# Tower of a language model: the state's product with the low part of the output weights over 128 rows instead of 64

## The reference, cut to what matters

```python
x = x + ssm(layernorm(x, ln1_s, ln1_b), A_diag, B, C, D)
h = layernorm(x, ln2_s, ln2_b)
x = x + gelu(h @ w1 + b1) @ w2 + b2

def ssm(x, a_diag, Bm, Cm, Dm):
    a = sigmoid(a_diag)              # 64 states
    u = x @ Bm                       # 256 -> 64
    # H[t] = a * H[t-1] + u[t], over the 512 tokens
    return H @ Cm + x @ Dm           # 64 -> 256 and 256 -> 256
```

## Time and profile before

| what | value |
|---|---|
| median of three runs | 2568.11 us (2562.83 to 2569.23) |
| the profiled execution | 2563.9 us, span 2562.1 us |
| TensorE, matmul busy | 85% of the span |
| VectorE busy | 63% |
| ScalarE busy | 52% |
| POOL busy | 28% |
| mean granted TensorE clock | 0.917 of full |

### The profile page before, as it was taken

The page is one execution under the profiler, slowest core; times in us unless marked ns, Lnnn a source line. Parts: engine busy times, 40 slices in busy tenths (PEclk is TensorE's granted clock), DMA queues, the critical chain, the costliest instruction groups (busy, mean ns, idle before and its releaser), DMA issues. The chain is left out here.

```text
span 2562.1 us, 43979 instructions
## 1 busy us (share of the span) xinstructions
PE 2165.1 (85%) x13087; PEld 1681.3 (66%) x13087; DVE 1613.2 (63%) x4682; ACT 1337.6 (52%) x2662; POOL 727.4 (28%) x837
## 2 busy tenths in 40 slices
PE   3899999999999999959885486389888889879892
PEld 2788888887888888846564365256555556555682
DVE  4555565556555655546774575687777778866335
ACT  3344454445444544435554565388777778811330
POOL 5111111111111111123354565022222222246452
PEclk8899999999999999979997698699889899989896
DMA  5720010001000000022222332522212222142556
GB/s 111 172 34 0 9 36 1 0 9 37 1 0 9 3 1 1 1 79 51 36 58 58 108 109 87 195 77 77 70 53 61 77 76 77 37 137 91 168 169 238
DMA packets 212265, 167.48 MB, mean 65 GB/s; under 512 B 109184, under 2 KB 170160, under 8 KB 212080
## 3 DMA queue, kind: packets, MB, share of 16 engines
q1 hardware_dynamic: 192608, 121.80, 18.0%
q0 software_dynamic: 14240, 38.35, 4.8%
q10 hardware_dynamic: 5232, 5.14, 0.6%
HBM read 91.07 MB, written 74.14 MB: 64 GB/s over the span
## 5 line engine op out<-in xcount | busy, mean ns | idle before, releaser
L633 PE MATMUL psum_o<-w_s,hid_s 128*128 128x256 f32 x3072 | 384.0, 284 | 19.0 <-ACT hid L437 19.0
L619 PE MATMUL psum_h<-xn2T_s,w_s 128*128 128x512 f32 x1536 | 389.1, 403 | 9.2 <-issue 4.6
L633 PEld LDWEIGHTS psum_o<-w_s,hid_s 128*128 128x128 f32 x3072 | 371.8, 188 | 26.9 <-issue 19.0
L436 ACT ACTIVATE hid_s<-psum_h,b 128x512 fp32r<-128x512 f32 x256 | 176.2, 688 | 391.3 <-PE psum_h L619 375.6
L619 PEld LDWEIGHTS psum_h<-xn2T_s,w_s 128*128 128x128 f32 x1536 | 282.6, 190 | 90.8 <-ACT hid L437 22.4
L2134 DVE CUSTOM_DVE_ANT_0 ra_z<-ra_psum_s,rhat 128x128 f32<-128x128 f32 (+3 forms) x512 | 228.6, 483 | 91.0 <-PE ra_psum_s L2249 76.7
L2084 ACT ACTIVATE ra_z<-ra_z,ra_nm 128x128 f32<-128x128 f32 (+3 forms) x512 | 244.7, 555 | 0.0
L2013 POOL TENSOR_SCALAR_AFFINE_SELECT ra_z<-ra_z 128x512 f32<-128x512 f32 x128 | 81.2, 635 | 453.6 <-DVE ra_z L2171 453.6
L2261 PE MATMUL ra_psum_p<-ident,ra_z 128*128 128x128 f32 x1280 | 185.0, 296 | 1.0 <-ACT turned L2076 1.0
L2249 PE MATMUL ra_psum_s<-ra_k_st,ra_q_st 48*128 48x128 f32 (+3 forms) x512 | 129.1, 371 | 64.3 <-DVE ra_mx L2134 48.0
L520 DVE TENSOR_TENSOR hid_s<-hid,hid_s 128x1024 fp32r<-128x1024 f32 x128 | 156.1, 1223 | 41.4 <-ACT hid L437 40.3
(11 more groups left out here) (394 smaller groups left out, 4280.1 us busy)
## 6 DMA issues: line engine op xcount, KB each, us to landing
ex_slots<-blank SPq DMA_DIRECT2D x1, 10296.0 KB, 33.7
ex_zT<-ex_slots SPq DMA_DIRECT2D x78, 132.0 KB
ex_rows<-ex_slots SPq DMA_DIRECT2D x8, 1056.0 KB, 9.6
w<-in_L_tok_w SPq DMA_DIRECT2D x8, 1024.0 KB
ra_scratch<-ra_hi SPq DMA_DIRECT2D x32, 256.0 KB
ra_scratch<-ra_lo SPq DMA_DIRECT2D x32, 256.0 KB
ra_q_st<-ra_scratch SPq DMA_DIRECT2D x128, 64.0 KB, 1.8
ra_k_st<-ra_scratch SPq DMA_DIRECT2D x128, 64.0 KB, 1.8
```

The source lines that it names most:

```text
L436: act.activation(hid_s[:, 0, m, :], psum_h[:, m % 2, :], ACT.Gelu, bias=b1[:, m:m + 1])
L619: mm = pe.matmul(psum_h[:, m % 2, :], w1_s[:, w_part, k, m * P:(m + 1) * P], xn2T_s[:, x_part, k, :], start=(n == 0 and k == 0), stop=(n = ...
L633: mm = pe.matmul(psum_o[:, t // 2, (t % 2) * D:(t % 2 + 1) * D], hid_s[:, h_part, m, t * P:(t + 1) * P], w2_s[:, w_part, m, :], start=(n = ...
```

## The change

The second matmul with the state reads all 128 rows of `state_s` and of the low part of C. The sum gains the product of the state's low part with C's low part. Nothing else is touched.

```diff
@@ -605,7 +605,7 @@
                     if t == 0:
                         pe.wait_ge(state_split, j + 1)
                     pe.matmul(out, state_s[:, tok], ssm_s[:, 0, SSM_C:SSM_D], start=False, stop=False)
-                    mm = pe.matmul(out, state_s[0:NS, tok], ssm_s[0:NS, 1, SSM_C:SSM_D], start=False, stop=True)
+                    mm = pe.matmul(out, state_s[:, tok], ssm_s[:, 1, SSM_C:SSM_D], start=False, stop=True)
                 mm.then_inc(y_done, 1)
```

## The result

The changed kernel takes 2509.09 us (median of four runs, 2505.58 to 2514.95), against 2565.99 us for the kernel before, measured beside it (2562.83 to 2569.23). The ratio is 0.9775, interval 0.9757 to 0.9793: 57 us or 2.2% faster. I had forecast 2519 us, with a range from 2509 to 2530. The direction and the mechanism in a plain step were right. The gain was forecast about 11 us too small: my sum was 45.6 us, the medians differ by 56.9. 2509.09 lies on the very edge of the range, and the ratio applied to 2565.99 gives 2508.3, outside it. The profiled execution took 2507.73 us.

What follows compares the result with a forecast made beforehand. The tower was taken as a chain of PE instructions that bounds the kernel. Steps 44.3 us plus prologue 1.3 us gave 45.6 us, 2563.9 - 45.6 = 2518.3 us, taken as 2519, range 2509 to 2530.

Steps and rivals of the forecast that it cites:

- terms 3 and 4: Tower: 31 step groups at 1.43 us give 44.3 us, two partly at lower clock gaining the same; prologue gives 1.3 us.
- Term 2: Plain step: surplus of 1.33 us in ssm_out and 0.10 us in the L619 behind it, together 1.43 us.
- term 5: What moves along: the 0.56 us hole stays; stages after the tower start 46 us earlier and are otherwise the same.
- rivals B and C: B: shared stationary tile keeps half the surplus, 2530 us, chance 0.09. C: row count sets no time, 2564 to 2568, 0.05.
- D: Tower: PE's shorter step loses the clock; two such steps eat the gain, three make 2589 us; chance 0.03.
- upper bound of 1.5 us more: The two lower-clock groups give some 1.5 us more if plain matmuls there were as short as 2.30 - 0.59 for eight.
- A: The forecast itself: ssm_out's surplus goes wholly, 2519 us, with 2510 to 2526 for scatter; chance 0.82.
- the rest: Outcomes beside the forecast and its three rivals; chance 0.01.

Runs made afterwards that it cites:

- eight visits: Against the adjacent kernel (two 64-row matmuls side by side): the first moved between the third and fourth L603; 2584.30 us, ratio 1.0244 to the kernel before.
- 96 rows: Against the kernel before: L608 alone, the last product, taken over 96 of the 128 rows; ratio 0.9768.
- four visits a step: Four passages from 128-row matmuls to 64 rows and back: the kernel before (2527.41 us again), or with L607 also cut to 64 rows, ratio 1.0012.
- the two with memsets: Against the changed kernel: 10 or 25 memsets on VectorE at the tower's end; 2479.83 and 2498.70 us.
- two visits a step: Against the kernel before: token tiles in pairs (0, 2) and (1, 3), each pair's two 64-row matmuls side by side; 2497.83 us, ratio 0.9887.
- 32 rows: Against the kernel before: L608 alone, the last product, taken over 32 rows; ratio 1.0001.

## Where the prediction was right, and where it failed

**What failed.** The sum of 45.6 us was 11 us short. The step that failed most clearly is in terms 3 and 4: the two ssm_outs at the lower clock were to give 1.4 us each, as in a plain step, with the clock taken as given. Together with the prologue I had 4.2 us for them, and the runs show 8.6. Term 2 was sized 0.08 us a step too small, 2.3 us in all. Some 5 us more came behind the tower, where term 5 had the stages "otherwise the same"; their cause stays open.

**The mechanism** in a plain step was right. The surplus around the 64-row matmul went wholly, in all 128 places, nothing waits in its stead, and rivals B and C are out: the pair with the shared stationary tile is 0.12 us apart as soon as both have 128 rows, and the order of the very same instructions moves the time by 56 us. D did not come; the clock of the plain tower is still full (of all kernels, only that with eight visits lost it between the early steps and the third layer), as the window of the changed kernel shows (columns as in the earlier trace rows):

```profile
320.00:530.00 210.00, 204.69 (x1341) 183.48 (x1342) 131.20 (x272) 106.85 (x166) 36.99 (x21) 1.00 0.03 8
```

Of the two rules that stood against each other, "TensorEngine Tiling (Array Packing)", Key Properties, of the Trainium skill says that a change of the tiling mode drains the engine. The runs side with it: the price goes with the visits, and 128 and 96 rows stand on the one side, 64 and 32 on the other. The drain itself no trace shows. The other rule of the Trainium skill, "TensorE: Matmul & The Clock Gate", LDWEIGHTS, has the load's time depend on columns and not on rows. The loads nearly agree (188 ns for 128 rows in the changed kernel, 183 for 64), but they were not the term that counted.

**Term 2, the surplus of a plain step,** was 1.43 us and measured 32.22 - 30.71 = 1.51. I had taken 0.122 us a matmul from L633. In ssm_out it is 0.96 / 8 = 0.120 us. On 29 plain ssm_outs that is 2.3 us.

**Terms 3 and 4, the early steps,** failed by their clock. I wrote that the two groups at the lower clock give "the same 1.4 us a step", because I took the clock as given. It isn't: with the gaps it stays low for longer. In five traces with four visits a step, the two ssm_outs of the first two steps took 16.0 to 18.2 us together, mean 17.1 (before 8.99 + 7.83). In six traces without visits (the changed kernel, 96 rows, and the two with memsets) they took 10.8 to 12.0, mean 11.3 (after 5.30 + 5.72). That is 5.8 us, where I had 2.9. From the first L592 to the fourth, prologue included, it is 117.0 to 122.6, mean 119.9 us, against 110.4 to 112.2, mean 111.3: 8.6 us where I had 4.2 of my sum in it. My upper bound of 1.5 us more did not cover that either. Rival D looked for the clock on the wrong side: the two ranges do not overlap, and the change gained there. The kernels between and beyond fit too: the two ssm_outs took 14.8 us with two visits a step and 23.6 with eight. Against twice a plain ssm_out of the same kernel (3.84, 4.49, 5.24 and 6.77 us) they are longer by 3.6, 5.8, 6.7 and 10.1 us for 0, 2, 4 and 8 visits. So the loss at the lower clock grows with the gaps.

The prologue alone was forecast with 1.3 us. From its L592 to the addition of y the five traces took 12.0 us in the mean and the six 10.5. But in the first pair it was 10.44 and 10.30, only 0.14 us: there the kernel before ran its first six L603 in 0.99 us, as at the full clock in the earlier trace rows, and the changed one in 1.65, as at the lower clock in the earlier trace rows. The mean bears the term out, and a single pair does not.

**Together** the early part and 29 plain ssm_outs give 29 x 1.51 + 8.6 = 52.4 us, against my 45.6. Measured at the tower's end were 51.0 us (1124.0 - 1073.0), 50.1 and 53.8 us in the three pairs of traces. The one stall before the third layer stayed in all traces, as 35.5 to 39.7 us for its step, and moves these differences by 2 to 4 us.

The chances have a slip too: A, B and the rest make 0.92 at most, where I wrote 0.93 for faster.

**Behind the tower** I had written "otherwise the same". They were not: 5.2 us in the first pair (1433.4 and 1428.2 us), 8.8 and 0.7 us in the others. Their instructions are the same, and the kernel before itself scatters from 1388.7 to 1397.9 us in the experiments; the kernel of eight visits, whose tower ends latest, had 1389.1. In the first pair the whole difference lies in the relative attention (623.1 and 617.8 us), which over all traces took 616.2 to 626.4 us. I read it mostly as scatter of the kernel before, which is not shown. But no trace without visits on the chips of the experiments exceeded 1392.2 us, and the medians of 57 and 59 us want some 5 to 7 us of it each time. Why the later stages should be quicker behind the changed tower is left open.

## What to carry to other kernels

A matmul over 64 or fewer rows between ones over 128 costs more than it saves: 0.38 us a visit here, three plain matmuls of 256 columns. Fill the rows up where the operands are there anyway, to 96 or more, or else put the small ones side by side. Look for starts that are further apart than their neighbours' behind an instruction of another row count, and not at the busy column. When PE has stood and runs at the lower clock, gaps of that kind were paid twice here, since the full clock also came back later.

## What the runs showed of the hardware

- 128 against 96 rows: no price; 128 against 64 rows: 0.38 us in and out, whether one or two matmuls are in between; 32 rows cost the same as 64, with one in between. About 0.1 us of it lies behind the first matmul in the small form.
- The lower clock (1.2 GHz) lasted 9 us and more in a stretch in which PE's recorded busy share was full (6.10 of 6.10 us), and was over by the third token tile in the same stretch without the gaps. The busy column did not tell them apart.
- The kernel before took 2566 us on one chip and 2526 on others. 23 us of this are the bf16 expert stage, in which PE is busy 114.5 of 160.5 us on the one and 103.4 of 137 on another.
